# Attention's output projection as three fp32r products, with its weight split in the first sequence and a smaller GpSimd DMA scratch

## The reference

```python
q = (x @ Wq.T + bq).reshape(B, N, HEADS, HEAD_DIM).transpose(0, 2, 1, 3)
k = (context @ Wk.T + bk).reshape(B, M, HEADS, HEAD_DIM).transpose(0, 2, 1, 3)
v = (context @ Wv.T + bv).reshape(B, M, HEADS, HEAD_DIM).transpose(0, 2, 1, 3)
attn = jax.nn.softmax(jnp.einsum('bhnd,bhmd->bhnm', q, k) * scale, axis=-1)
out = jnp.einsum('bhnm,bhmd->bhnd', attn, v)
out = out.transpose(0, 2, 1, 3).reshape(B, N, C)
return out @ Wo.T + bo
```

## Time and profile before

| What | Value |
|---|---|
| Runs of the kernel | 2155.63 us median, 2154.73 to 2157.56 |
| The profiled execution | 2156.37 us, span of its instructions 2154.6 us |
| Busy shares of the span | PE 93%, VectorE 66%, ScalarE 57%, GpSimd 18% |
| Mean granted PE clock | 0.967 of 2.4 GHz |
| 0 to 940 us (Mamba) | PE 875.45 busy of 940, VectorE 710.40, ScalarE 399.35 |
| 940 to 1873 us (attention) | PE 883.65 busy of 933, VectorE 547.24, ScalarE 693.85 |
| 1873 to 2154 us (experts) | PE 242.76 busy of 281, VectorE 156.71, ScalarE 130.06 |

### The profile page before, as it was taken

One profiled execution on the slowest core, in us unless ns is written; L12 is line 12 of the kernel. 1 busy time (PEld: TensorE's weight loads), 2 busy tenths in 40 slices (PEclk: granted clock), 3 DMA queues, 4 the chain that ended last, 5 costly groups with the idle time before them and its releaser, 6 DMA issues. The chain is left out here.

```text
span 2154.6 us, 39863 instructions
## 1 busy us (share of the span) xinstructions
PE 2001.9 (93%) x13356; PEld 1318.8 (61%) x13356; DVE 1414.4 (66%) x2811; ACT 1223.3 (57%) x3068; POOL 389.6 (18%) x595
## 2 busy tenths in 40 slices
PE   6999999999999999858999999999999999689988
PEld 4767676767676767434555555555655564378853
DVE  6978787878787868535556565656565656265438
ACT  4435353444444444217868787877777777246514
POOL 0111101111111110231212212122222222100006
PEclk8999999999999999888999999999999999889999
DMA  6122222222222222242333232334343322161157
GB/s 205 53 58 78 59 77 59 77 53 82 49 87 49 87 47 69 79 127 80 98 81 113 75 111 69 118 81 118 80 113 82 100 82 70 66 233 59 59 177 272
DMA packets 120289, 200.94 MB, mean 93 GB/s; under 512 B 22945, under 2 KB 44449, under 8 KB 120097
## 3 DMA queue, kind: packets, MB, share of 16 engines
q1 hardware_dynamic: 110880, 179.46, 27.4%
q0 software_dynamic: 9216, 18.89, 3.5%
HBM read 117.53 MB, written 29.88 MB: 68 GB/s over the span
## 5 line engine op out<-in xcount | busy, mean ns | idle before, releaser
L1579 ACT ACTIVATE a_shared<-a_shared,a_mx 128x512 f32<-128x512 f32 x512 | 340.8, 669 | 50.6 <-DVE a_mx L1627 50.5
L1572 ACT ACTIVATE a_probs<-a_scores 128x512 f32<-128x512 f32 x512 | 291.9, 603 | 109.6 <-PE a_scores L1730 107.3
L1627 DVE TENSOR_REDUCE a_mx<-a_shared 128x1 f32<-128x512 f32 x512 | 318.3, 681 | 30.2 <-PE a_shared L1714 29.8
L925 PE MATMUL m_proj<-m_xt_hi,link 128*128 128x512 f32 x576 | 245.2, 426 | 21.2 <-DVE m_xt_lo L649 10.5
L1730 PE MATMUL a_scores<-a_qs,a_ks 98*128 98x512 f32 x512 | 217.7, 434 | 21.5 <-ACT a_probs L1572 17.7
L1714 PE MATMUL a_shared<-a_ks,a_qs 96*128 96x512 f32 x512 | 220.2, 441 | 15.8 <-ACT a_shared L1579 11.6
L926 PE MATMUL m_proj<-m_xt_lo,link 128*128 128x512 f32 x576 | 233.2, 405 | 0.0
L927 PE MATMUL m_proj<-m_xt_hi,link 128*128 128x512 f32 x576 | 232.1, 403 | 0.0
L1067 PE MATMUL m_outp<-m_wout,m_g 128*128 128x512 f32 x512 | 226.0, 600 | 2.7 <-issue 2.7
L1688 PE MATMUL a_shared<-link 128*128 128x512 f32 x768 | 189.8, 400 | 18.5 <-POOL a_ks L1519 15.7
L460 ACT ACTIVATE m_acc<-m_proj,m_cb,m_cw 128x512 f32<-128x512 f32 x72 | 58.1, 818 | 254.4 <-PE m_proj L927 253.7
(11 more groups left out here) (243 smaller groups left out, 3327.2 us busy)
## 6 DMA issues: line engine op xcount, KB each, us to landing
m_dec<-step_decay SPq DMA_DIRECT2D x64, 256.0 KB, 4.0
a_qs<-link SPq DMA_DIRECT2D x256, 64.0 KB, 2.1
m_ce<-run_decay SPq DMA_DIRECT2D x128, 112.0 KB, 3.6
a_ks<-a_k_hi POOLq DMA_DIRECT2D x192, 64.0 KB, 2.4
e_x<-x SPq DMA_DIRECT2D x11, 1024.0 KB, 5.6
m_xt_in<-x_t_in SPq DMA_DIRECT2D x8, 1024.0 KB, 8.1
m_x_tok<-x_in SPq DMA_DIRECT2D x8, 1024.0 KB, 6.5
x<-m_x_tok SPq DMA_DIRECT2D x32, 256.0 KB, 2.2
```

The costliest lines, as they stand in the source:

```text
L925: pe.matmul(bank[:, :], wh, xt_hi[:, k, :], start=(k == 0), stop=False)
L1572: act.activation(probs[:, n % 2, h, :], scores[t.score_bank(n, h)][:, :], ACT.Exp, scale=-1.0).then_inc(exp_ready, 1)
L1579: act.activation(scored[:, :], scored[:, :], ACT.Exp, scale=-1.0, bias=mx[:, i % 2, j, h:h + 1], accum_out=den[:, i, j, h:h + 1]).then_inc ...
L1627: dve.tensor_reduce(mx[:, i % 2, j, h:h + 1], bank(what)[:, :], AX.X, ALU.min).then_inc(mx_ready, 1)
```

## The change

- The output projection is made in three parts, as q, k and v are: `o_hi` x `wo_hi`, `o_hi` x `wo_lo`, `o_lo` x `wo_hi`, twelve fp32r matmuls a tile in place of four float32 ones.
- `norm` writes its product into `inv_rows`. A new VectorE step `osplit` makes `o_hi` and `o_lo` from it, in the third unit of the next group (in the second unit for the last group, ahead of its output tiles). The value bias is added there, as a column per channel, since attention weights sum to one; `v` becomes a plain copy.
- The weight lands in `x_tok`'s memory. VectorE splits it in four steps `wo`, in units 2, 3, 6 and 7 of the first turn. The first load of `x_tok` and the output tiles wait for them.
- Less memory is set aside for GpSimd's DMA descriptors: 2048 bytes a partition.

```diff
@@ attention_order, parts_of
+WO_UNITS = [2, 3, 6, 7]
...
         if u == 0:
             put("norm", group, 0, 0, d)
+        if u == (2 if n >= TT else 1):
+            put("osplit", group, 0, 0, d)
...
+    first_turn = []
+    for step, d in steps:
+        if d >= 0:
+            first_turn.append((step, d))
+        if d == 0 and step[0] == "st" and step[3] == AG - 1 and TT * step[1] + step[2] in WO_UNITS:
+            first_turn.append((("wo", WO_UNITS.index(TT * step[1] + step[2]), 0, 0), 0))
...
-            "first": [(step, d) for step, d in steps if d >= 0],
+            "first": first_turn,
@@ attention_stage, memory
-        w_o = sb("wo", [P, KT, DM])
-        brow = sb("brow", [P, 2, DM])
+        wo_hi = sb("wo_hi", [P, KT, DM], F32R)
+        wo_lo = sb("wo_lo", [P, KT, DM], F32R)
+        brow = sb("brow", [P, DM])
+        bvcol = sb("bvcol", [P, KT])
...
-        o = sb("o", [P, KT, SEQ])
+        o_hi = sb("o_hi", [P, KT, SEQ], F32R)
+        o_lo = sb("o_lo", [P, KT, SEQ], F32R)
@@ SyncE
-                for i in range(2):
-                    sp.dma_start(brow[:, i, :], b_row[i].partition_broadcast(P)).then_inc(small_in, 16)
-                sp.dma_start(w_o[:, :, :], woT.rearrange("(k p) n -> p k n", p=P)).then_inc(small_in, 16)
+                sp.dma_start(brow[:, :], b_row[1].partition_broadcast(P)).then_inc(small_in, 16)
+                sp.dma_start(bvcol[:, :], b_row[0]).then_inc(small_in, 16)
+                sp.dma_start(x_tok[:, :, :], woT.rearrange("(k p) n -> p k n", p=P)).then_inc(small_in, 16)
...
                 elif kind == "load":
+                    if t.first():
+                        sp.wait_ge(wo_s, 2 * KT)
@@ VectorE
                     dve.wait_ge(v_done, t.at(TT, i + 1))
-                    if part == "start" and i == 0:
-                        dve.wait_ge(small_in, N_SMALL)
...
-                    dve.tensor_tensor(v[:, i, :], bank(what)[:, :], brow[:, 0, :], ALU.add).then_inc(v_ready, 1)
+                    dve.tensor_copy(v[:, i, :], bank(what)[:, :]).then_inc(v_ready, 1)
...
                     dve.wait_ge(av_done, t.at(UNITS, TT * (i + 1)))
+                    dve.tensor_tensor(inv_rows[:, :], o_bank[:, :], inv_rows[:, :], ALU.mult).then_inc(o_ready, 1)
+                elif kind == "osplit":
                     if i == 0 and not t.first():
                         dve.wait_ge(out_done, t.at(TT, 0))
-                    dve.tensor_tensor(o[:, i, :], o_bank[:, :], inv_rows[:, :], ALU.mult).then_inc(o_ready, 1)
+                    dve.wait_ge(o_ready, t.at(KT, i + 1))
+                    dve.tensor_scalar(o_hi[:, i, :], inv_rows[:, :], bvcol[:, i:i + 1], None, ALU.add
+                                      ).then_inc(o_split, 1)
+                    dve.wait_ge(o_split, t.at(2 * KT, 2 * i + 1))
+                    dve.scalar_tensor_tensor(out=o_lo[:, i, :], in0=inv_rows[:, :], scalar=bvcol[:, i:i + 1],
+                                             in1=o_hi[:, i, :].bitcast(F32), op0=ALU.add, op1=ALU.subtract
+                                             ).then_inc(o_split, 1)
+                elif kind == "wo":
+                    dve.wait_ge(small_in, N_SMALL)
+                    dve.tensor_copy(wo_hi[:, i, :], x_tok[:, i, :]).then_inc(wo_s, 1)
+                    dve.wait_ge(wo_s, 2 * i + 1)
+                    dve.tensor_tensor(wo_lo[:, i, :], x_tok[:, i, :], wo_hi[:, i, :].bitcast(F32), ALU.subtract
+                                      ).then_inc(wo_s, 1)
@@ PE
                     if i == 0:
-                        pe.wait_ge(o_ready, t.at(KT, KT))
+                        pe.wait_ge(wo_s, 2 * KT)
+                        pe.wait_ge(o_split, t.at(2 * KT, 2 * KT))
                     take(part, what, t)
                     for k in range(KT):
-                        ins = pe.matmul(bank(what)[:, :], o[:, k, tile], w_o[:, k, :], start=(k == 0),
-                                        stop=(k == KT - 1))
+                        for n, (op, wp) in enumerate(((o_hi, wo_hi), (o_hi, wo_lo), (o_lo, wo_hi))):
+                            ins = pe.matmul(bank(what)[:, :], op[:, k, tile], wp[:, k, :], start=(k == n == 0),
+                                            stop=(k == KT - 1 and n == 2))
@@ kernel
-    nc = bacc.Bacc("TRN2", target_bir_lowering=False, num_devices=1)
+    nc = bacc.Bacc("TRN2", target_bir_lowering=False, num_devices=1, dynamic_dma_scratch_size=2048)
```

More of the change, by code:

```diff
@@ L1369, in attention_stage @@
         small_in = sem("small_in")
+        wo_s = sem("wo_s")
+        o_split = sem("o_split")
         const = sem("const")
@@ L1535, in step @@
                     pool.tensor_tensor(x_tok[:, :, :], x_tok[:, :, :],
-                                       brow[:, 1, :].unsqueeze(1).to_broadcast([P, TT, DM]), ALU.add).then_inc(xb_ready, 1)
+                                       brow[:, :].unsqueeze(1).to_broadcast([P, TT, DM]), ALU.add).then_inc(xb_ready, 1)
                 elif kind == "out":
@@ L2402, in lay_out @@
         "b_qk": np.stack([i[t + "bq"], i[t + "bk"]]).reshape(2, KT, P).transpose(2, 0, 1),
-        "bv": i[t + "bv"], "bo": i[t + "bo"],
+        "bv": i[t + "bv"].reshape(KT, P).T, "bo": i[t + "bo"],
         "gamma": i[f + "ln_gamma"], "beta": i[f + "ln_beta"], "mu": i[f + "mu"].reshape(DM, SLOTS),
```

## The result

The changed kernel takes **2145.38 us** (median of 6 runs, 2144.53 to 2147.86), the kernel before 2155.18 in the same comparison (6 runs, 2151.86 to 2160.87): ratio 0.9954, 95% interval 0.9940 to 0.9968. The forecast was 2143.3 with a range of 2135.5 to 2150.5, "faster". Side, range and size hold. The profiled executions are 2156.37 and 2145.03 us, spans 2154.6 and 2143.3, mean clock 0.967 and 0.966.

What follows compares the result with a forecast made beforehand. PE (TensorE) was taken to set the turn, busy 105.66 of 107.5 us. Terms -18.5 - 2.8 + 5.8 + 1.4 + 1.3 + 0.5 = -12.3 from 2156.37 gave 2144.1, as a median 2143.3 us, range 2135.5 to 2150.5.

Steps and rivals of the forecast that it cites:

- Output tiles: PE's output projection: a three-part tile takes 2.85 us for 3.54, sparing 2.64 us a sequence, 18.5 us in seven turns.
- The first tile and the late maxima: Units 1 to 3: the split delays unit 2's maxima and ScalarE; the tile's 0.69 and 0.14 more lost, 5.8 us.
- Tiles two to four: Other output tiles in each turn: no lateness found, since ScalarE waits for PE behind them; 1.95 us a turn.
- Rival B: VectorE's 5.1 us a turn mostly come back, tiles two to four pay half: 2150 us, chance 0.15.
- The unseen 0.2 a turn: Allowance in each turn for lateness that the prediction couldn't see, 1.4 us in all.
- SyncE's slack for stack 0: SyncE's fill for the next sequence: slack 1.3 us against a delay up to 1.3, counted as 0.
- The weight's split: VectorE's casts and subtractions in the first sequence: one cast waits beside GpSimd, 0.5 us once, between 0 and 3.
- The ring: GpSimd's smaller descriptor scratch: bound below nothing, 4.5 us of slack at the tightest fill; no cost in the sum.
- rival C: GpSimd's 2048-byte scratch makes transfers land in pairs, fills 8.6 us longer: slower, 2191 us, chance 0.05.
- The tail: Last sequence's end: four shorter tiles spare 2.8 us, the uncovered split before them costs 1.3.
- A: PE alone decides: late maxima find slack and all four tiles pay, gain 20.0, 2135.6 us, chance 0.18.
- four passes for fp32: Skill's rule for output tiles: three parts cost 0.75 of a tile, some 28 us saved; measured rows preferred.

Runs made afterwards that it cites:

- later groups: Second and third groups of runs, the unaltered changed kernel against the kernel before on the same chip: 2145.17 us, ratio 0.9936, and 2146.74 us, ratio 0.9945.
- the doubled split: Changed kernel with the last group's subtraction into `o_lo` done twice, the second writing the same values: 2158.50 us, ratio 0.9995 to the kernel before.
- the version with both edits: Changed kernel with the last group's split moved to unit 0 and PE waiting for one group's split at a time: 2140.25 us (0.9913), again 2141.32 (0.9921).

## Why the prediction was right, and where its parts were off

**Output tiles.** Spared were 0.64 on the first, 1.26 on the next two and 0.64 on the fourth, 2.54 a sequence and not 2.64. The term was some 4% of it too large: the first matmul behind an `av` block costs 0.11 more than the rest, and the row that the tile was priced by has none of that.

**The first tile and the late maxima.** That the split of unit 1 makes the maxima and ScalarE's run late, and PE wait for it, is shown four ways: moving the split takes away 0.36 a turn, leaving it out takes away the same, adding it alone to the fp32 kernel costs the same, and a second subtraction costs 0.80 more. The size was off, and one step with it. ScalarE's run ended 0.35 late and not 0.5, and the first tile gave 0.52 on its own and not 0.41 at most. The 0.41 was read from the end of a record. In the changed kernel ScalarE's two copies begin at 1336.44 and the next instruction at 1337.49, 1.05 behind; 1.05 behind the copies of the earlier trace rows is 1342.43, so the slack until 1343.00 was 0.57. ScalarE thus started on unit 3 0.21 earlier than before, where the prediction had 0.1 later. The wait that it named at the third score matmul of unit 3 wasn't there; the fourth came 0.38 behind the third, 0.28 before. So of its 0.69, 0.52 - 0.35 = 0.17 remained, where the prediction had it all lost and 0.14 more. That is 0.31 a turn.

**Tiles two to four** gave 1.90 of the forecast 1.95. Rival B's half did not happen. **The unseen 0.2 a turn** was 0.30 in this profile. Part of it can be named: PE waits in unit 13 for the stack that SyncE fills for group 1 of the next sequence,

```profile
1625.97 0.49 PE L1742 MATMUL a_shared<-a_ks,a_qs 96*128 96x512 f32 x1 [0.79 <-DMA a_qs<-link]
```

twice in six turns here, two to four such waits in other profiles, 0.1 to 0.9 us each; it is there with the splits left out too, and in none of the three profiles with fp32 tiles. The prediction worked out SyncE's slack for stack 0 only. At this place there was hardly any: in the profiles with fp32 tiles PE comes 2.2 to 2.3 us behind the end of the last issue, and the median landing in the kernel before is 2.1. A turn was thus 1.73 shorter on the mean, 1.61 forecast.

**The weight's split** cost nothing (forecast 0.5, bounds 0 to 3): the first sequence is 0.12 shorter, and the four casts took 0.42 each, also the one beside GpSimd's issues. The second began 0.13 after GpSimd had begun to write descriptors (VectorE's row, then GpSimd's):

```profile
1015.89 0.42 DVE L1674 CAST a_wo_hi<-a_x_tok 128x512 fp32r<-128x512 f32 x1
...
1015.76 3.08 POOL L1460 DMA_DIRECT2D a_ks<-a_k_hi  x6 [31.37 <-PE a_scores L1758]
```

By the rule of a lock held for a whole instruction (the Trainium skill, SBUF — State Buffer, SBUF: two separate sides) the cast would wait for the rest of the issue under way, by estimate 0.37 us of its 0.50; the row shows no wait. It was GpSimd that lost a little there: its six issues took 3.08 where they took 2.94, and the one beside the cast 0.64 in place of 0.50, also in the second profile of the changed kernel. **The ring** cost nothing, rival C was wrong, and the pause that came more often was 0.56 and not 2.9.

**The tail** was 1.3 for the split, measured 1.35, and 2.8 for four tiles. What the prediction missed is the clock: the first tile there lost 1.6 us of it, so that from its start to the last tile's only 0.39 was spared in place of some 1.9. In the last sequence's units 6 to 11, where PE's instructions were the same, most of another 2.46 were lost, with three clock falls where the kernel before had one. Against that the stage ahead of attention was 1.45 shorter in this profile. The clock first rises to 1.00 at 13.5 us there and at 15.0 in the kernel before; in the 13 profiles, all with the same code up to this point, it rises between 12.9 and 16.0, and the start of attention's first `av` moves with it. That is no part of the change.

**The sum.** Forecast 12.3; the profiles differ by 11.3, attention and what follows by 9.9, the medians by 9.8 (later groups by 12.6 and 11.1). Larger gains in the turns (10.38 + 2.51 = 12.9 for 11.3) were taken back by the clock in the last sequence and the tail (4.0, forecast 0). Two errors of opposite sign made the number better than its parts; that is luck.

**The rivals.** A, with all four tiles paying, is what the kernel becomes once the split stands in unit 0 and the tail doesn't wait: 0.9913 to 0.9921 measured, 2135.6 / 2155.6 = 0.9907 forecast. In this kernel it didn't happen: one place of four had no cover. The Trainium skill's four passes for fp32 (FP8 and Floating Point Precision, TensorE Precision Notes) would make the three parts 0.75 of a tile, by estimate; measured is 2.90 / 3.54 = 0.82, so the trace doesn't bear that out.

**What stays open.** Whether the clock falls more in the last sequence with shorter tiles. All 13 profiles have three long waits of PE there, fp32 tiles or not: 2.2 us for ScalarE, 1.1 for a transfer of negated maxima, 1.3 for ScalarE. In eleven a fall stands beside the first of them, in the other two, longer ones, beside the last; which of the waits have a fall changes from profile to profile. In the some 60 us ahead of the tail the profiles with fp32 tiles lost 1.7, 3.4 and 6.8 us of full clock (each fall 1.7), the ten with three-part tiles 3.4 to 6.8. Two profiles of one kernel differ by 1.7 of this, the changed kernel's first (5.1) and the one before (1.7) by 3.4; the ranges overlap, so the 2.46 above may be in large part chance. Whether the tail's fall needs the three-part tile behind the wait, or missed the fp32 tile by chance, isn't settled either. Open too is why the stack's transfer sometimes landed 3.2 us behind the end of its issue, which is what makes PE wait.

## What to carry to other kernels

Before an operation is put into a list of steps, look at the idle time of its engine right at that place, and at who reads what it delays: three of four splits cost nothing, the fourth cost 0.36 us a turn, and the same instructions some 5 us earlier were free. Where a fast engine waits for a last piece at the end of a stage, let it start on the pieces that are there. And price a lengthened wait of TensorE with what the clock may do behind it: here 1.35 us of waiting cost 2.9, and in the doubled split 0.8 cost 2.2 in four turns of six.

## What the runs showed of the hardware that I had not expected

In attention's turns and tail the falls of the clock were alike. One lasted some 3.4 us at 0.50 and cost 1.7 us of full speed; at times two or more followed one another directly. Most came behind waits of PE: behind the 2.24 us of the tail in four profiles of five, behind 3.03 there in the doubled split, behind 1.34 in four turns of six; none behind the 0.88 and 0.93. The wait alone doesn't decide: in the kernel before one of 1.57 at 953 us had none behind it, and in both profiles of the version with both edits one fall stands in a turn (1174.9 and 1504.2 us) with no wait over 0.32 in the 10 us ahead of it.

PE stops once in each profile at the jump back of the loop, between its two iterations; the trace names nothing that it waits for. The stop was 0.52 to 1.27 us in ten profiles, with no fall, and 1.53, 1.84 and 1.85 in three, each with a fall behind it. Here is one of the last kind, from the kernel before with the small scratch, and a window of it:

```profile
1436.74 0.50 PE L1714 MATMUL a_shared<-a_ks,a_qs 96*128 96x512 f32 x1 [1.53 <-issue]
```

```profile
1439.00:1441.00 2.00, 2.00 (x34) 1.43 (x37) 2.00 (x4) 1.68 (x4) 0.00 (x0) 0.50 0.29 72
```

Such an event moves a single run by 2 to 4 us, as much as the edits that were tested: runs of one kernel differed by up to 12 us. The intervals between like blocks of two traces, good to 0.05, decided what the times couldn't.
